# Two graph layers in one kernel: node rows made earlier in the tick, a store cut into 28 parts, and a new order in hop 0

## The reference

```
x: (50000, 64)   src, dst: (25000,)   edge_attr: (25000, 64)   edge_weight: (25000,)
h = relu(layernorm(x))
x = x + relu(relu((h + segment_sum(h[src], dst)) @ W1 + b1) @ W2 + b2)
h = relu(layernorm(x))
deg  = segment_sum(1, dst);   dinv = deg > 0 ? deg ** -0.5 : 0
norm = dinv[src] * dinv[dst] * edge_weight
Q = relu(h @ Wq + bq);  K = h @ Wk + bk;  V = h @ Wv + bv     (8 heads of 8)
hop 0:     Kj = relu(K[src] + edge_attr);  M = segment_sum(norm * outer(Kj, V[src]), dst)
hop 1, 2:  M = segment_sum(norm * M[src], dst)
after each hop:  H = Q . M, shortened to norm sqrt(8) where longer
result = x + V * hopwise[0] + sum over hops of hopwise[hop + 1] * H
```

## Time and profile before

| | |
|---|---|
| median of 3 runs | 1816.89 us (1813.88 to 1824.14) |
| profiled execution, its own time | 1815.59 us |
| span of its instructions | 1812.7 us |
| mean granted TensorE clock | 0.86 of full speed |
| busy: DVE | 1488.8 us (82% of the span) |
| busy: PE, POOL, ACT | 1345.3, 1193.0, 1015.2 us |

### The profile page before, as it was taken

One profiled execution on the slowest core, in us unless ns is written; L12 is line 12 of the kernel. 1 busy time (PEld: TensorE's weight loads), 2 busy tenths in 40 slices (PEclk: granted clock), 3 DMA queues, 4 the chain that ended last, 5 costly groups with the idle time before them and its releaser, 6 DMA issues. The chain is left out here.

```text
span 1812.7 us, 22165 instructions
## 1 busy us (share of the span) xinstructions
PE 1345.3 (74%) x5794; PEld 840.3 (46%) x5794; DVE 1488.8 (82%) x3207; ACT 1015.2 (56%) x2815; POOL 1193.0 (66%) x1185
## 2 busy tenths in 40 slices
PE   3666778788888985777777277778577898877772
PEld 3455666665666664454544033333233344455551
DVE  5866777789989886799999799999456788699992
ACT  4556878768878875455554255555355556333330
POOL 7775666616665531777773577777477777777776
PEclk9787898879978877798998589888799999988886
DMA  4394333334655554699998588888435554466650
GB/s 126 77 51 123 102 104 102 91 94 132 149 134 141 133 135 92 213 323 319 320 318 293 177 288 305 307 309 299 152 98 159 146 160 135 128 174 175 173 152 17
DMA packets 280787, 313.83 MB, mean 173 GB/s; under 512 B 168577, under 2 KB 198137, under 8 KB 268118
## 3 DMA queue, kind: packets, MB, share of 16 engines
q1 hardware_dynamic: 223734, 246.39, 45.3%
q0 software_dynamic: 56928, 66.04, 14.6%
HBM read 214.54 MB, written 161.32 MB: 207 GB/s over the span
## 5 line engine op out<-in xcount | busy, mean ns | idle before, releaser
L924 PE MATMUL bank<-product,ident 128*128 128x512 f32 (+1 forms) x800 | 383.3, 637 | 134.9 <-DVE product L1278 134.9
L533 POOL DMA_INDIRECT state<-state_hop,slot_of_src x392 | 395.6, 1009 | 126.1 <-issue 108.5
L703 ACT ACTIVATE bank<-state,norm 128x512 f32<-128x512 f32 x392 | 251.1, 679 | 254.9 <-DMA state<-state_hop,slot_of_src 221.6
L1278 DVE TENSOR_TENSOR product<-bank,queries 128x512 f32<-128x512 f32 x392 | 261.2, 687 | 90.0 <-ACT bank L703 88.3
L924 PEld LDWEIGHTS bank<-product,ident 128*128 128x128 f32 x800 | 160.9, 206 | 356.0 <-issue 182.7
L495 POOL DMA_INDIRECT x_edges<-in_x,dst_tiles x196 | 199.5, 1018 | 156.9 <-DVE x_edges L1188 97.0
L509 POOL DMA_INDIRECT row_of_src<-node_rows,pos_int x196 | 195.2, 996 | 122.2 <-DMA node_rows<-row_new 62.8
L495 POOL DMA_INDIRECT x_edges<-in_x,src_tiles x196 | 203.1, 1036 | 95.8 <-issue 54.4
L549 POOL DMA_INDIRECT out<-rows,dst_out x196 | 193.1, 985 | 59.7 <-issue 50.0
L831 PE MATMUL bank<-dst_steps,from_here 128*128 128x197 f32 x392 | 98.6, 406 | 101.7 <-ACT row_no L645 75.2
L1276 DVE SCALAR_TENSOR_TENSOR acc<-acc,same_as_before,bank 128x512 f32<-128x512 f32 x196 | 145.2, 741 | 15.9 <-ACT bank L703 15.1
(11 more groups left out here) (220 smaller groups left out, 3033.0 us busy)
## 6 DMA issues: line engine op xcount, KB each, us to landing
state_hop<-acc SPq DMA_DIRECT2D x98, 1024.0 KB, 4.7
x_nodes<-in_x SPq DMA_DIRECT2D x49, 256.0 KB, 3.6
src_row<-in_src_row SPq DMA_DIRECT2D x49, 256.0 KB, 3.6
out<-out_rows SPq DMA_DIRECT2D x49, 256.0 KB
dst_row<-in_dst_row SPq DMA_DIRECT2D x49, 256.0 KB, 4.5
kv_rows<-kv SPq DMA_DIRECT2D x49, 256.0 KB, 3.5
gg<-head_sums SPq DMA_DIRECT2D x98, 128.0 KB
kv_back<-kv_rows SPq DMA_DIRECT2D x49, 256.0 KB
```

Source lines behind the costliest of these rows:

```text
L533: pool.indirect_dma_start(out=mg[u % 4][:, k, :], out_offset=None, in_=d_m[hop - 1], in_offset=bass.IndirectOffsetOnAxis(ap=sidx[:, t:t + ...
L703: act.activation(pw[t % len(pw)][:, :], mg[u % 4][:, k, :], ACT.Copy, scale=wn12[:, t:t + 1]).then_inc(weighted, 1)
L924: ins = ten.matmul(ph[:, 0:k * D].rearrange("p (c j) -> p c j", j=HD), ident[:, :], part, start=(r == 0), stop=(r == HD - 1))
L1278: vec.tensor_tensor(ihj(pr[m % 2][:, u % 2 * EH + k, :]), ihj(pw[t % len(pw)][:, :]), over_j(Q[:, t, :]), ALU.mult).then_inc(multiplied, 1)
```

## The change

The program for SyncE stores the row tails in 28 parts of seven columns, one in each tick from 12 to 39. GpSimd waits for all 28 where it waited for the one.

On VectorE the node rows (line 1176) move within their tick from behind the result rows to a place right behind the reciprocal and factors. Their wait for the second product moves with them.

In hop 0 VectorE makes the first two outer products of the older unit before it waits for the rows of the newer one; the three tiny instructions follow one place later each. The slot computation moves behind the last unit's sums. There VectorE also waits for the last queries. On ScalarE the copy of the values goes ahead of the queries.

```diff
+TAIL = 7
+TAIL_AT = {12 + i: i * TAIL for i in range(T // TAIL)}
...
-                if g == 12:
+                if g in TAIL_AT:
+                    c = slice(TAIL_AT[g], TAIL_AT[g] + TAIL)
                     sync.wait_ge(tail_set, 2)
-                    sync.dma_start(by_slot(d_tab)[:, :, D:TW], tail[:, :, :]).then_inc(tail_kept, 16)
+                    sync.dma_start(by_slot(d_tab)[:, c, D:TW], tail[:, c, :]).then_inc(tail_kept, 16)
...
-            pool.wait_ge(tail_kept, 16)
+            pool.wait_ge(tail_kept, 16 * len(TAIL_AT))
...
                     own.add(ins)
+                    own.sync()
+                    act.activation(kvz[u % 3][:, :, D:2 * D], parts[:, :, 1, :], ACT.Copy).then_inc(v_done, 1)
                     act.wait_ge(q_mm, u + 1)
                     for k in range(EH):
                         t = u * EH + k
                         ins = act.activation(Q[:, t, :], pQz[:, k * D:(k + 1) * D], ACT.Relu, scale=dinv[:, t:t + 1])
                     ins.then_inc(q_done, 1)
-                    own.sync()
-                    act.activation(kvz[u % 3][:, :, D:2 * D], parts[:, :, 1, :], ACT.Copy).then_inc(v_done, 1)
...
                 else:
                     select(1)
+                m = DENSE_AT.get(g - 4)
+                if m is not None:
+                    vec.wait_ge(mm2_d, m + 1)
+                    wait(vec, res_d, m - RX + 1)
+                    vec.scalar_tensor_tensor(flat(x1d[m % RX][:, 0, :, :]), pbd[:, :], 0.0, flat(xn[m % RX][:, 0, :, :]),
+                                             ALU.max, ALU.add).then_inc(x1_d, 1)
...
-                m = DENSE_AT.get(g - 4)
-                if m is not None:
-                    vec.wait_ge(mm2_d, m + 1)
-                    wait(vec, res_d, m - RX + 1)
-                    vec.scalar_tensor_tensor(flat(x1d[m % RX][:, 0, :, :]), pbd[:, :], 0.0, flat(xn[m % RX][:, 0, :, :]),
-                                             ALU.max, ALU.add).then_inc(x1_d, 1)
...
-                if 0 <= n < CU:
-                    vec.wait_ge(row_in[n % RT], landed(n, n % RT, RT, 16 * EH))
-                    own.add(vec.tensor_tensor(dv[:, o], tg[n % RT][:, :, D + 1], spm[:, o], ALU.is_equal))
                 if 0 <= u < CU:
                     vec.wait_ge(k_done, u + 1)
                     vec.wait_ge(v_done, u + 1)
                     outer(u, 0)
                     outer(u, 1)
                 if 0 <= n < CU:
-                    own.sync()
-                    own.add(vec.tensor_tensor(dv[:, o], dv[:, o], tg[n % RT][:, :, D], ALU.mult))
+                    vec.wait_ge(row_in[n % RT], landed(n, n % RT, RT, 16 * EH))
+                    own.add(vec.tensor_tensor(dv[:, o], tg[n % RT][:, :, D + 1], spm[:, o], ALU.is_equal))
                 if 0 <= u < CU:
                     wait(vec, m0_kept[u % 3], landed(u - 3, u % 3, 3))
                     join(u, 0)
                     outer(u, 2)
                 if 0 <= n < CU:
                     own.sync()
-                    vec.tensor_tensor(wn0[:, o], dv[:, o], wpm[:, o], ALU.mult).then_inc(wn_set, 1)
+                    own.add(vec.tensor_tensor(dv[:, o], dv[:, o], tg[n % RT][:, :, D], ALU.mult))
                 if 0 <= u < CU:
                     join(u, 1)
                     outer(u, 3)
+                if 0 <= n < CU:
+                    own.sync()
+                    vec.tensor_tensor(wn0[:, o], dv[:, o], wpm[:, o], ALU.mult).then_inc(wn_set, 1)
+                if 0 <= u < CU:
                     join(u, 2)
                     join(u, 3)
-                if g == D0 - 2:
+                if g == D0 - 1:
                     vec.wait_ge(wn_set, CU)
...
                 if g == D0 - 1:
+                    vec.wait_ge(q_done, CU)
                     for b in range(3):
                         vec.wait_ge(kv_kept[b], landed(CU - 1, b, 3))
```

## The result

The changed kernel takes 1750.57 us (median of 4 runs, 1748.66 to 1756.38), the kernel before in the same comparison 1820.52 (4 runs, 1813.88 to 1828.31). The ratio is 0.962, 95% interval 0.957 to 0.967. The profiled execution took 1748.99 us, span 1746.5: 66.2 us less span than before. The granted clock is 0.87 in the mean, where it was 0.86.

What follows compares the result with a forecast made beforehand. Source stage held by engines waiting for each other, destination stage nearly VectorE-bound. Gains 17.9 (tail store) + 29 (source) + 2 (patch) + 6 (destination) + 3.2 (hop 0) = 58.1 us off 1815.6; median forecast 1758, range 1726 to 1792.

Steps and rivals of the forecast that it cites:

- signs of being wrong: Product waits in most pairs, destination pairs over 12.7 us, more output-store waits on VectorE, or granted clock above 0.95.
- The 2 us a transfer: Tail store: fixed cost per transfer from the skill page; 28 parts would be an estimated 56 us instead of 2.
- Rival C: Tail store: parts hold SyncE's queue in pieces and the 17.9 us stays spread out; 1776 us, chance 0.08.
- The ping-pong: Source stage: VectorE's late node rows delay ScalarE's square, then searches and root; VectorE idles 2.18 us a pair.
- with 0.88 granted, a quarter of the time is at half: Source stage: half-clock waits for TensorE's product add 0.7 us, making a pair 11.1 us instead of 10.41.
- rival B: Both stages: the clock rises, source pairs take 10.7 us, destination gains the whole 28.2; 1730 us, chance 0.15.
- 10.7 us, about the GpSimd figure: Source stage: lower bound on a pair's time, near GpSimd's 10.6 us a pair; would gain 33 us.
- GpSimd is no limit there: Source stage: GpSimd needs 5.3 us a unit, 10.6 a pair, and runs up to ten units ahead.
- The four earlier pairs: Source stage: four more pairs, run ahead of the stall beside preparation work, gain 0.7 us each, 2.8 together.
- two or three slow pairs should become ordinary: Destination stage: fewer half-clock pairs as TensorE loses part of its idle; helps justify a 6 us gain.
- Rival D: Both stages: nearly every pair's moved instruction waits 3.56 us for an unfinished product; slower, 1894 us, chance 0.04.
- Patch: Serial stretch between the source and destination stages: node rows moved early gain 2 us, bounds 0 to 5.

Runs made afterwards that it cites:

- e1: Kernel before with only the tail store in 28 parts of seven columns: 1803.3 us, ratio 0.985.
- e8: Kernel before with two added unread products on TensorE at each odd source-stage tick from tick 11: 2095.26 us, ratio 0.998, on a slower chip.
- e2: Kernel before with only the node rows moved right behind the factors, both stages; one tail store, old hop 0: 1784.1 us, ratio 0.976.
- e4: Changed kernel with two added unread products on TensorE at the head of each odd destination-stage tick: 1718.63 us, ratio 0.940.
- e5: Changed kernel with node rows in their old place and two added unread products a pair, destination stage only: 2081.23 us beside 2101.9, ratio 0.988.
- e3: Changed kernel with the node rows early in the source stage only, in their old place from tick 49 on: 1749.45 us, ratio 0.957.
- e12: Changed kernel with the destination stage's node rows behind the second layer's normalised rows, nothing added: 2071.58 us beside 2080.9, ratio 0.995.
- middle order: Node rows behind the second layer's normalised rows in the destination stage of the changed kernel; the 312.5 us stage is e12's, ratio 0.995.

## Why the prediction was right, step by step

The total (58.1 forecast, 66.2 measured by the span) came out because two errors of opposite sign partly cancel: the source stage gave 20 us more than forecast, the destination stage 13 less. That the sum lies so near is luck. Three of the prediction's own signs of being wrong came: a clock above 0.95 in the source stage, and in the destination stage a wait for the product in 16 of 24 pairs and pairs longer than 12.7 us.

**Tail store: right.** 17.9 forecast, 18.2 measured, and 18 alone in e1. The Trainium skill's advice to coalesce (DMA: Bandwidth & Descriptors, "Rules for kernel authors") doesn't hold for this store: nobody waits for a part, and the queue behind a part is free in half a microsecond. The 2 us a transfer that the prediction took from the Trainium skill ("Anatomy of one DMA") are given there for transfers that GpSimd issues, and SyncE issued these. Rival C falls with the same rows.

**Source stage: mechanism right, size too small (29 against 48.8).** The ping-pong was read rightly: square, root and search each lose their wait. The mis-sized term is the step "with 0.88 granted, a quarter of the time is at half", which kept the old clock for the new order and so charged a pair 0.7 us of waits. The order also shortened TensorE's idle before each second search (2.3 to 3.9 us in most pairs before, 1.4 to 1.9 after), the clock went to 1.00, and a pair is VectorE's own 10.2 us and not 11.1: here rival B's mechanism was true. By the shortest pairs of e8 the clock without the order wins nothing; what the order would win at the old clock no run shows. The bound "10.7 us, about the GpSimd figure" was no bound for 16 pairs, but "GpSimd is no limit there" was too sure. It takes some 11.5 us for two units now, which is a pair's worth, and a lead of five units, not ten, carried the difference and was down to one at the end. The four earlier pairs, put at 0.7 each beside preparation work, gave 10.9 us together, 8.3 of them by the order alone (e2).

**Destination stage: wrong in sign (6.8 lost, 6 gained in the forecast).** Its prices were right: the wait in a half-clock pair is 3.36 to 3.55 us (3.56 forecast), and such a pair is longer than before, 15.4 to 15.6 us against 14.6. Its count of slow pairs before was one too high: the trace has seven idles of 2.42 to 2.45 us, not eight, and six pairs of 14.6 us. The step that failed is the count, "two or three slow pairs should become ordinary". Leave the few short pairs at the stage's ends aside. Before there are 14 pairs at 12.72 us and 6 at 14.6; after, 8 at 11.96, 5 at 13.4 and 8 at 15.5. Were all at their ordinary length, the stage would have gone from 296 to 278 us, 18 won. But the surcharge went from 6 x 1.9 = 11 us to 5 x 1.5 + 8 x 3.5 = 36, some 24 lost, and the difference is about the measured 7. Two things were missed. Falls of the clock became more (from 8, two of them shallow, to 13), since the order wins time for VectorE and does not take away TensorE's idle at the head of the odd tick. And shallow falls, which cost nothing before, cost 1.5 us: the late order had slack behind the product, and the early one has none (waits of 1.31 to 1.39 us in these five pairs). e4 shows both: with the idle filled the clock never falls, no long pair is left, and the stage takes 280 us. How many falls an order gets also varies: e2, with the same early order, had 11 and took 307.9 us. So the loss of 6.8 us is of the size by which this stage moves between kernels that are alike in it; what is sure is that the forecast gain didn't come. Rival D's mechanism was at work here, in 16 waits and not in all.

By the Trainium skill (TensorE: Matmul & The Clock Gate, "Why this matters for your kernels") TensorE's idle gaps must be kept short, or the clock falls. The trace agrees in the source stage, 1.00 where the gap shrank to 1.4 to 1.9 us. In the destination stage the clock fell behind gaps of 1.8 us as well, shorter than those that the page warns of, and stayed at 1.00 throughout only where they were filled (e4, e5).

**Patch and hop 0: about right.** 3.2 for 2, and 2.3 for 3.2; hop 0's share is within what kernels of one order differ by, and only its first 0.8 to 0.9 us are shown.

## What to carry to other kernels

When an instruction moves, read what its new wait costs at each of TensorE's two levels and how many pairs will be at which; that count follows from TensorE's gaps in the new order, not from the old mean clock. Where one engine is the bound and TensorE idles a little in each round, try products that nobody reads in that gap: here they were worth nearly half as much as the change itself, on the one chip where this could be read. Look at the engine that feeds the stage too: a lead that was built up hides that it is slower. A transfer of very many tiny pieces is best cut when something sits behind it in its queue, and a stall that ends at a fixed landing hides what is won ahead of it, so the two edits must be judged together.

## What the runs showed of the hardware

- In the changed kernel 13 idle times of TensorE of 1.8 us, each at the head of a pair, were each followed by a pair at 0.87 or 0.67 of the full clock; in e2 five such idles of 1.6 to 1.85 us were not. 1.88 us of unread products in their place gave 1.00 over 280 us (e4) and a stage of 279.9 us for 314.0; the kernel was 31 us faster than e3.
- One store of 25,088 pieces of 8 bytes holds its queue for 28.9 us; the same bytes in 28 stores, about 5 us apart, mostly take 0.43 us each to issue (0.38 to 0.45 in e1; in the changed kernel three take 0.72, 1.08 and 3.22), and the next load 0.33.
- The same program takes 1821 and 1826 us in two comparisons and 2081 and 2102 in two others, on other chips. The single instructions are as long (an outer product 690 ns in both); what is added are waits that the trace ascribes to no instruction, mostly of readers of TensorE's results (316 to 518 us in each of e5 to e12, none in the others). An order with little slack behind these results seems to suffer more (destination stage 312.5 us in the middle order against 304.7 in the old). What delays them wasn't found, nor whether it belongs to the chip or to the hour.
